# Shared groups of a mixture-of-experts layer split five and three around the experts, with the additions of the routed rows spread over twelve chunks

## The reference, cut to what matters

```python
scores = softmax(xt @ gate_w.T)
_, idx = top_k(scores + gate_bias, 2)
weights = take_along_axis(scores, idx, axis=1)
y = 0
for e in range(8):
    gate_e = sum(where(idx == e, weights, 0.0), axis=1)
    h = silu(xt @ w1[e].T) * (xt @ w3[e].T)
    y = y + gate_e[:, None] * (h @ w2[e].T)
z = silu(xt @ sw1.T) * (xt @ sw3.T) @ sw2.T
return (y + z).reshape(shape)
```

## Time and profile before

| | |
|---|---|
| median of three runs | 578.78 us (577.35 to 578.97) |
| the profiled execution's own time | 576.23 us |
| its span | 574.5 us |
| TensorE busy | 530.0 us (92% of the span) |
| VectorE busy | 428.4 us (75%) |
| ScalarE busy | 316.1 us (55%) |
| GpSimd busy | 274.3 us (48%) |
| mean granted clock of TensorE | 0.975 of full |

### The profile page before, as it was taken

How to read it: one execution, slowest core, us unless ns; L and a number is a source line. 1 busy time by engine, 2 the same in 40 slices (tenths; PEclk the granted TensorE clock), 3 DMA queues, 4 the chain that set the end, 5 groups by cost and what they waited for, 6 DMA issues and landing times.

```text
span 574.5 us, 11248 instructions
## 1 busy us (share of the span) xinstructions
PE 530.0 (92%) x3362; PEld 469.5 (82%) x3362; DVE 428.4 (75%) x1138; ACT 316.1 (55%) x693; POOL 274.3 (48%) x582
## 2 busy tenths in 40 slices
PE   5989999989999996689999979999999999998984
PEld 5986799988689995568888868888888888887863
DVE  6879989578998798856778645666666666664896
ACT  3649998165999824135554424555555555554321
POOL 4157600082550160077777704777777777675000
PEclk9979999989999999879999998999999999999999
DMA  8999800000030006522222212333333333331995
GB/s 261 319 281 145 3 1 2 1 1 1 2 110 1 1 1 218 223 103 99 100 101 97 104 43 71 103 112 104 103 113 103 103 113 103 103 103 58 337 357 184
DMA packets 57401, 63.03 MB, mean 110 GB/s; under 512 B 15008, under 2 KB 50720, under 8 KB 57344
## 3 DMA queue, kind: packets, MB, share of 16 engines
q1 hardware_dynamic: 48944, 43.74, 28.3%
q0 software_dynamic: 6480, 17.90, 8.7%
q10 hardware_dynamic: 1920, 0.67, 0.5%
HBM read 30.65 MB, written 31.65 MB: 108 GB/s over the span
## 4 chain that ended last, share of the span: by engine, by line
PE 54%; DVE 5%; issue 2%; ACT 1%; DMA 0%; DVEq 0%
PE bank L1516 16%; PE bank L1517 15%; PE bank L1518 15%; PE bank L1601 3%; PE bank L1617 3%; PE bank L1525 1%; DVE YG L1423 1%; DVE h_lo L1319 0%; DVE X L1433 0%; DMA gbias<-in_gate_bias_dram 0%; DVE hf L1315 0%; DVE X L1415 0%; DVE XN L1297 0%; DVE X L1374 0%; DVE red L1398 0%
## 5 line engine op out<-in xcount | busy, mean ns | idle before, releaser
L1207 POOL DMA_INDIRECT token_out<-YS,to_row x71 | 71.7, 1010 | 48.4 <-DVE back L1485 45.0
L1170 POOL DMA_INDIRECT slots_in<-X,slot x64 | 66.6, 1041 | 41.2 <-DVE slot L1399 22.0
L980 PE MATMUL a_bank<-VO,E_hi 128*128 128x266 f32 x272 | 78.7, 289 | 3.2 <-DVE E_lo L752 3.2
L984 PE MATMUL a_bank<-VO,E_lo 128*128 128x266 f32 x272 | 77.7, 285 | 0.0
L982 PE MATMUL a_bank<-VO,E_hi 128*128 128x264 f32 x272 | 77.6, 285 | 0.0
L1474 DVE TENSOR_TENSOR hr<-bank,sr 128x256 f32<-128x256 f32 x71 | 30.1, 424 | 59.8 <-ACT sr L1259 59.8
L1516 PE MATMUL bank<-W_hi,XST_hi 128*128 x142 | 62.5, 440 | 0.5 <-DVE XST_lo L1490 0.5
L1259 ACT ACTIVATE sr<-bank 128x256 f32<-128x256 f32 x71 | 27.3, 384 | 63.6 <-PE bank L1518 63.6
L1516 PE MATMUL bank<-XT_hi,sw_hi 128*128 128x512 f32 x128 | 52.3, 409 | 6.4 <-DVEq L1290 3.4
L752 DVE TENSOR_TENSOR E_lo<-E,E_hi 128x512 fp32r<-128x512 f32 (+1 forms) x80 | 54.3, 713 | 4.9 <-ACT E_hi L531 4.9
L1518 PE MATMUL bank<-W_hi,XST_lo 128*128 x142 | 56.4, 397 | 0.0
(11 more groups left out here) (245 smaller groups left out, 1606.2 us busy)
## 6 DMA issues: line engine op xcount, KB each, us to landing
XS<-slots_in SPq DMA_DIRECT2D x71, 131.0 KB, 2.1
slots_in<-blank SPq DMA_DIRECT2D x7, 1179.0 KB, 16.5
YG<-token_out SPq DMA_DIRECT2D x16, 512.0 KB, 9.0
W_raw<-in_wT_dram SPq DMA_DIRECT2D x8, 768.0 KB, 10.0
X<-in_x_dram SPq DMA_DIRECT2D x8, 512.0 KB, 7.8
out_dram<-X SPq DMA_DIRECT2D x32, 128.0 KB, 2.8
token_out<-YS,to_row POOLq DMA_INDIRECT x71, 2.5
slots_in<-blank SPq DMA_DIRECT2D x1, 1048.0 KB, 15.2
```

Source lines behind the costliest of these rows:

```text
L980: pe.matmul(O_ps[Q % 2][j][:, 0:XW + 2], E_hi[:, n % NE, cols], VO[:, kt, 0:XW + 2], start=(kt == 0), stop=False)
L984: mm = pe.matmul(O_ps[Q % 2][j][:, 0:XW + 2], E_lo[:, n % NE, cols], VO[:, kt, 0:XW + 2], start=False, stop=(kt == qt))
L1170: pool.indirect_dma_start(out=xs, out_offset=bass.IndirectOffsetOnAxis(ap=slot[k][:, t:t + 1], axis=0), in_=X[:, t, 0:RW], in_offset=None) ...
L1207: pool.indirect_dma_start(out=ys, out_offset=bass.IndirectOffsetOnAxis(ap=to_row[:, i:i + 1], axis=0), in_=YS[:, i % NYS, :], in_offset=No ...
```

## The change

HALF becomes 5: groups 0 to 4 (chunks 0 to 19) stand ahead of the experts, groups 5 to 7 (chunks 20 to 31) behind them. Both tables are written anew for the twelve chunks: the pairs of group 0 are added in the fourth chunk (number 3), then each chunk up to number 10 carries one group's addition and the next group's pairs, and number 11 none. The place of a group follows HALF. The waits that name HALF (lines 1141, 1585, 1641) follow it too.

```diff
         N_XTL = KC
         N_EARLY = 3
-        HALF = 6
+        HALF = 5
 
         def place(G):
 
...
         def group_to_add(n):
 
-            return {2: [0], 3: [1], 4: [2], 5: [3, 4], 6: [5], 7: [6]}.get(n - MC * HALF, [])
+            return {4: [0], 5: [1], 6: [2], 7: [3], 8: [4], 9: [5], 10: [6]}.get(n - MC * HALF, [])
 
         def pairs_to_add(n):
 
-            return {1: [0], 2: [1], 3: [2], 4: [3, 4], 5: [5], 6: [6], 7: [7]}.get(n - MC * HALF, [])
+            return {3: [0], 4: [1], 5: [2], 6: [3], 7: [4], 8: [5], 9: [6], 10: [7]}.get(n - MC * HALF, [])
```

## The result

The changed kernel took 585.63 us (median; the kernel before 578.88 beside it), a ratio of 1.0119 with an interval of 1.0063 to 1.0175: slower, and 0.1 us from the forecast of 585.5. One execution, at 864 us, was disturbed and is not in the ratio; the three others took 580.1, 584.6 and 586.7 us. They lie 6.6 us apart, so a hit within 0.1 us is luck: the size of the effect is known to about 3 us either way. The profiled execution was the quickest of the three, and its span is only 3.9 us over that of before. First the profile page's lines on the span, on the engines' busy time, and on the shares of the engines in the chain of work that ended last.

What follows compares the result with a forecast made beforehand. TensorE bounds the expert stage, VectorE is fuller behind it, and the scatters gate the experts' start. -7.4 us ahead and +14.1 behind sum to +6.7, so 585.5 us on the median's scale, range 583.0 to 589.0.

Steps and rivals of the forecast that it cites:

- The gate: Ahead of the experts: row loads wait for all scatters to land, so the expert stage starts 7.7 us earlier, not 17.6.
- The low end of the range: Whole kernel: 0.8 us off the scatters, no clock cost and no new waits at the groups: +4.3 us, so 583.0.
- Rival 1: Ahead of the experts: scatters keep up and experts start once TensorE is free: -3.5 us, 575.3, faster; chance 0.03.
- The clock: Start-up of the experts: idle TensorE drops to 1.2 GHz, costing +0.6 us, bounds 0 to +2.
- register loads: Start of the experts: TensorE's own register loads are already done in the new order, gaining 0.3 us of 0 to 0.5.
- The walk along VectorE: Behind the experts: chunk-by-chunk timing with the pitches of the trace makes this stage 14.1 us longer.
- Rival 4: Behind the experts: spreading the additions relieves nothing, since shared outputs themselves cause the waits: +10.2 us, 589.0; chance 0.02.
- rival 3: Low clock holds through the experts' start-up, or VectorE lacks cover behind the experts; together +10 us, 588.8; chance 0.12.
- Rival 2: Ahead of the experts: scatters run freer with less work beside them: +1.5 us instead of +6.7, 580.3; chance 0.04.

Runs made afterwards that it cites:

- the condition with the hold-up: The changed kernel again in a later set, TensorE waiting on its own instruction issue during the scatters: 643.27 us against 646.56 for the kernel before, ratio 0.994.
- both gated traces of five groups: The changed kernel with SyncE's first loads also waiting for 35 small GpSimd fills: ratio 1.0114; with 33 matmuls added in the idle time: 1.0077.
- the busy matmuls: 33 matmuls nothing reads, put in TensorE's idle time ahead of the experts, on the changed kernel with 35 GpSimd fills delaying loads: 652.22 us against 654.5.
- the packed tables: The changed kernel with additions packed into the first seven chunks behind the experts, group 6 alone waiting for chunk 9: 644.28 us, ratio 0.9962.

## Why the prediction was right

**The gate.** "SyncE's load still goes at about 331.67" was right in kind and 0.8 us too late: from the first scatter it came at 87.9 us and not 88.6. The low end of the range had the same 0.8 us, but from scatters that run more freely, and they did not: from first to last start they took 85.2 us, against 84.9. The gain lies behind the last one, 2.6 us from its start to SyncE's load (325.35 to 327.95) where it had been 3.8. The prediction made the 3.8 of 0.96 for the scatter and 2.6 for the landing; but the landing is counted from the scatter's start, and the slowest took 4.4 us before and 3.5 after. Why landings came sooner is open. The step from the load to the rows, 2.3 us forecast, took 2.16. Rival 1, that the experts start as soon as TensorE is free, was wrong in the first measurement. In the condition with the hold-up it came true, with the time that I had given it: -3.5 us forecast, ratio 0.994 or -3.9 measured. But it did so for another reason than the rival's: the scatters kept their pace of 1.28 us, and it was TensorE that fell behind them, which I had not weighed.

**The clock.** The net of this term was +0.3, made of 0.6 for the clock and 0.3 back for register loads. The gain was real: TensorE starts 0.47 us behind the start of the normalised rows where it was 0.89, so 0.4 us, and the same in both gated traces of five groups. The clock was undersized: the stage as a whole took 1.1 us more, which leaves 1.5 for the clock, and the busy matmuls give 1.1 by trace and 2.3 by medians, just over the bound of 2. TensorE worked at 1.2 GHz for six microseconds, three more than before, where the forecast had one more. But the same stage took 188.2 us, 0.9 more than before, in the later trace that had no idle time to expose, so how much of the 1.1 is the clock's stays open. This net term was 0.8 us too small and the time to SyncE's load 0.8 us too long, and the two offset each other: that the sum is closer than its terms is luck too.

**Behind the experts.** The walk along VectorE gave +14.1 and the trace has +14.3. All three of its new waits are there. The largest (0.5, chunk 24's shared output) is 0.36 of idle time and 0.16 of overlap. The 0.4 of chunk 27 and the 0.1 of chunk 28 are the late starts at 556.11 and 560.50, 0.3 and 0.1 us by TensorE's pace, though no idle time is written beside them. That spreading earns its keep is shown by the packed tables. Rival 4, that spreading relieves nothing, is out; the half of rival 3 that has VectorE without cover, too: short of the last chunk's natural wait of 0.80 there is none over half a microsecond.

**Rival 2** (freer scatters) did not happen at all: 15 of the 64 took over 1.1 us, against 14 before, though one group's work less lay beside them.

**The chances.** 0.92 on slower was for the condition of the trace of before. None of my cases had that the same two kernels could stand the other way round in another condition, as they did in the later sets.

## What to carry to other kernels

Work that seems to be in the way may be what hides a second chain: before moving it, look for what became ready shortly before the hand-over (here a load issued 10 us ahead of its first use) and take the later of the two ends. Where a vector engine carries side work between two steps of a pipeline, walk it chunk by chunk with the pitches of the trace, and use both sides of the step that the tensor engine waits for. In rows of matmuls look at the distance of the starts as well as at the idle time in brackets, since an overlap can hide a wait. And before believing the sign of a 1% effect, see it again at another time and on another chip.

## What the runs showed of the hardware that I had not expected

In all twelve later traces, on four chips, TensorE's matmuls waited for issue, started multiples of 0.7 us apart, from some 20 us behind the first of the 64 scatters until some 8 us behind the last, for about 50 us in all. ScalarE and VectorE stood still with it (VectorE for 36 us in one piece in the trace shown), while GpSimd kept its pace of a scatter every 1.28 us; in the first two traces nothing of it shows. Eight scatters fewer moved the end of it by 10 us, so the scatters sustain it. What is held up, and why only in the later sets, is open; so is whether it would go with scatters that are spaced differently, which wasn't tried. And VectorE pays for GpSimd's sums beside it: its normalising took 4.28 us for four tiles instead of 1.38, three times as long, while GpSimd's sums took 1.29 us in the median and at most 1.84.
